# Linear attention with slots and eight experts on one core: roundings of batches 1 to 3 placed earlier, first loads and first two products woven

## The reference

```python
q, k, v = heads(x @ Wq), heads(x @ Wk), heads(x @ Wv)
s = clip(heads(x @ Ws), -32, 32)                  # 64 slots per head
z = cumlogsumexp(s); g = exp(z_before - z); p = exp(s - z)
hk = hk * g + k p^T;  ok = (q * scale) @ hk       # scan over tokens
pv = softmax(ok)
hv = hv * g + p v^T;  o = pv @ hv                 # scan over tokens
o = o * rsqrt(mean(o * o) + 1e-5) * g_norm * silu(x @ Wg)
x = layernorm(x + o @ Wo)
h = relu(x @ W1 + b1);  alpha = softmax(h @ W2 + b2)
x = layernorm(x + sum_k alpha_k * ((x @ V_k^T) @ U_k^T))
```

## Time and profile before

| | us |
|---|---|
| median of 3 runs | 1321.6 (1321.35 to 1323.63) |
| the profiled execution | 1321.39 |
| its span | 1319.6 |
| TensorE busy in it | 1304.1 (99%) |
| VectorE, ScalarE, GpSimd busy | 935.2, 534.8, 426.1 (71%, 41%, 32%) |

### The profile page before, as it was taken

One profiled execution on the slowest core, in us unless ns is written; L12 is line 12 of the kernel. 1 busy time (PEld: TensorE's weight loads), 2 busy tenths in 40 slices (PEclk: granted clock), 3 DMA queues, 4 the chain that ended last, 5 costly groups with the idle time before them and its releaser, 6 DMA issues.

```text
span 1319.6 us, 21997 instructions
## 1 busy us (share of the span) xinstructions
PE 1304.1 (99%) x8652; PEld 1151.3 (87%) x8652; DVE 935.2 (71%) x1887; ACT 534.8 (41%) x1551; POOL 426.1 (32%) x390
## 2 busy tenths in 40 slices
PE   9999999999999999999999999999999999999998
PEld 7888888898888888888888988888888888988886
DVE  5677777777777777777777777777777777766654
ACT  5434443444434433344334434444334433632321
POOL 3413342244223331334125422343123423442211
PEclk9999999999999999999999999999999999999999
DMA  6002100010000100010001000010000110000000
GB/s 231 33 32 65 49 17 1 1 45 13 17 1 25 33 17 1 19 39 17 1 1 49 9 17 1 24 33 17 1 25 25 65 34 1 1 0 33 31 34 33
DMA packets 33847, 36.04 MB, mean 27 GB/s; under 512 B 3536, under 2 KB 24016, under 8 KB 33744
## 3 DMA queue, kind: packets, MB, share of 16 engines
q1 hardware_dynamic: 33744, 34.64, 8.3%
HBM read 30.43 MB, written 4.19 MB: 26 GB/s over the span
## 4 chain that ended last, share of the span: by engine, by line
PE 95%; DVE 3%; ACT 1%; DMA 0%; issue 0%; SPq 0%; POOLq 0%; POOL 0%; DVEq 0%
PE p L1044 15%; PE p L1045 15%; PE p L1046 15%; PE t L1095 5%; PE o L1260 3%; PE s L1148 2%; PE xb L1213 2%; PE o L1198 2%; PE o L1196 2%; PE t L1260 2%; PE p L1148 2%; PE s L1572 2%; PE s L1573 2%; PE s L1574 2%; PE xb L1170 2%; PE o L1195 2%
## 5 line engine op out<-in xcount | busy, mean ns | idle before, releaser
L1044 PE MATMUL p<-wvg_hi,xt_hi 128*128 128x512 f32 x512 | 203.2, 397 | 0.0
L1045 PE MATMUL p<-wvg_lo,xt_hi 128*128 128x512 f32 x512 | 200.1, 391 | 0.0
L1046 PE MATMUL p<-wvg_hi,xt_lo 128*128 128x512 f32 x512 | 199.5, 390 | 0.0
L558 POOL TENSOR_TENSOR orstd<-ovar,minus_half 128x8 f32<-128x8 f32 x32 | 52.4, 1638 | 431.9 <-DVE ovar L995 431.9
L520 POOL TENSOR_TENSOR s_lo<-sums,s_hi 128x512 fp32r<-128x512 f32 x64 | 83.1, 1299 | 225.5 <-ACT s_hi L647 225.5
L1044 PE MATMUL p<-xt_hi,wsqk_hi 128*128 128x512 f32 x372 | 148.0, 398 | 2.1 <-DVE xt_lo L892 1.7
L1045 PE MATMUL p<-xt_lo,wsqk_hi 128*128 128x512 f32 x372 | 145.4, 391 | 0.0
L1046 PE MATMUL p<-xt_hi,wsqk_lo 128*128 128x512 f32 x372 | 145.1, 390 | 0.0
L622 ACT ACTIVATE v_tok<-p 128x256 f32<-128x256 f32 x128 | 49.6, 388 | 217.7 <-PE p L1046 216.7
L904 DVE COPY hv<-xb 64x128 f32<-64x128 f32 x192 | 55.1, 287 | 95.4 <-PE xb L1213 94.0
L1046 PEld LDWEIGHTS p<-wvg_hi,xt_lo 128*128 128x128 f32 x512 | 96.1, 188 | 20.9
(11 more groups left out here) (278 smaller groups left out, 3549.0 us busy)
## 6 DMA issues: line engine op xcount, KB each, us to landing
raw<-in_L_attn_Wv SPq DMA_DIRECT2D x32, 128.0 KB, 2.3
raw<-in_L_attn_Wg SPq DMA_DIRECT2D x32, 128.0 KB, 2.9
raw<-in_L_attn_Wo SPq DMA_DIRECT2D x16, 256.0 KB, 2.9
acc<-in_L_attn_hidden_states SPq DMA_DIRECT2D x4, 1024.0 KB, 5.6
out<-acc SPq DMA_DIRECT2D x16, 256.0 KB, 2.0
acc<-in_turned SPq DMA_DIRECT2D x3, 1024.0 KB, 8.9
raw<-in_L_attn_Ws SPq DMA_DIRECT2D x8, 256.0 KB, 2.9
raw<-in_L_attn_Wq SPq DMA_DIRECT2D x8, 256.0 KB, 2.9
```

Source lines behind the costliest of these rows:

```text
L558: nc.gpsimd.tensor_tensor(orstd[:], ovar[:], minus_half[:], ALU.pow).then_inc(orstd_done, 1)
L1044: nc.tensor.matmul(out_, lh, rh, start=(k == 0), stop=False)
L1045: nc.tensor.matmul(out_, lh, rl, start=False, stop=False)
L1046: last = nc.tensor.matmul(out_, ll, rh, start=False, stop=(k == n - 1))
```

## The change

The change has six parts. Nothing that is computed changes; eight transposes that fill time are left out.

1. SyncE issues the first loads woven: Ws, x tile 0, Wq, x tile 1, Wk, x tiles 2 and 3. ScalarE rounds them in that order; four pieces of Wv and Wg move by a place among the first features.
2. TensorE computes slots and queries together, tile by tile (`first_slots_and_queries`), with one group of four filling transposes instead of three. The transposes of e stand before the scores, and vg0 waits for the pieces of Wv and Wg one by one.
3. In cell 0, ScalarE rounds the last two groups of Wo behind the keys and then batch 2 (`x_high(act, 2)`); VectorE makes the second half of `xt_lo` of batch 1 before the exponential's result, the clip of the slots before `keep_values(2)`, and the first half of `xt_lo` of batch 2 at the cell's end.
4. In cell 1, ScalarE rounds batch 3 instead of batch 2; VectorE makes the second half of batch 2 where all four tiles stood, and the first half of batch 3 behind the additions. In cell 2 only the second half of batch 3 is left.
5. In the last cell `w2_low` moves behind the x1 tiles 1 to 3.
6. In the tail the four products of the last rows that go to p0 and p1 run before the wait for the hidden tile, and the two that go to OB after it.

```diff
         def sync_part(sp):
             xv = x.rearrange("b (n p) d -> b p n d", p=P)
             xtv = XT.rearrange("b (k p) t -> b p k t", p=P)
-            load_piece(sp, 0, name_of(0), 0)
             for kt in range(KT):
+                if kt < 3:
+                    load_piece(sp, 0, name_of(kt), kt)
                 sp.dma_start(acc[:, kt, :], xtv[0, :, kt, :]).then_inc(x0_in[kt], 16)
-            for i in (1, 2):
-                load_piece(sp, 0, name_of(i), i)
...
-        def rows_high(act, J):
-            act.wait_ge(wo_scaled, 2 * (J + 1))
-            if J > 0:
+        def rows_high(act, J, parts=range(4)):
+            if 0 in parts:
+                act.wait_ge(wo_scaled, 2 * (J + 1))
+            if 0 in parts and J > 0:
                 act.wait_ge(a_done, B * J)
-            for k, (where, src) in enumerate(row_groups):
+            for k in parts:
+                where, src = row_groups[k]
                 if k == 2:
                     act.wait_ge(wo_summed, 4 * (J + 1))
...
-        def x_high(act, b):
-            for kt in range(KT):
+        def x_high(act, b, parts=range(KT)):
+            for kt in parts:
                 act.wait_ge(*((x0_in[kt], 16) if b == 0 else (x_in[b], 16)))
                 nc.scalar.activation(xt_hi[b][:, kt, :], acc[:, b * CH + kt, :], ACT.Copy).then_inc(xt_hi_done, 1)
...
-            if 0 < cell.b < B - 1:
-                x_high(act, cell.b + 1)
+            if cell.b == 1:
+                x_high(act, 3)
...
-            if wo_J is not None:
+            if wo_J == 0:
+                rows_high(act, 0, (0, 1))
+            elif wo_J is not None:
...
+            if first(cell):
+                rows_high(act, 0, (2, 3))
+                x_high(act, 2)
...
         def scalar_part(act):
-            split_high(act, 0, 0, None)
-            x_high(act, 0)
-            split_high(act, 0, 1, None)
-            split_high(act, 0, 2, None)
+            for kt in range(KT):
+                if kt < 3:
+                    split_high(act, 0, kt, None)
+                x_high(act, 0, (kt,))
             split_high(act, 0, 3, None)
+            split_high(act, 0, 4, None)
             slots_scalar(act, Cell(None, 0))
+            split_high(act, 0, 5, None)
             queries_scalar(act, Cell(None, 0))
-            split_high(act, 0, 4, None)
-            split_high(act, 0, 5, None)
+            split_high(act, 0, 6, None)
             keys_scalar(act, Cell(None, 0))
-            split_high(act, 0, 6, None)
...
                                     ALU.subtract).then_inc(ok_less_top, 1)
-            if not first(cell):
+            if first(cell):
+                x_low(dve, 1, (2, 3))
+            else:
...
-                x_low(dve, cell.b + 1)
+                x_low(dve, cell.b + 1, (2, 3))
...
             keep_values(1)
-            if first(cell):
-                x_low(dve, 1, (2, 3))
             gate_vector(dve, cell, 3)
             if not first(cell):
                 add_c(dve, cell)
                 add_u3(dve, cell)
-            keep_values(2)
+            if cell.b == 1:
+                x_low(dve, 3, (0, 1))
             if cell.b == CELLS - 2:
                 dve.wait_ge(added, CELLS - B + 1)
                 car.norm1_tile(dve, 0, 0)
                 car.norm1_tile(dve, 0, 1)
+            if first(cell):
+                slots_vector(dve, nxt)
+                keep_values(2)
+                sums_vector(dve, nxt)
+                inverse_vector(dve, nxt)
+            else:
+                keep_values(2)
             if last:
-                car.w2_low(dve)
                 car.x_low(dve, 0, 0, X1[0])
-            if not last:
+            elif not first(cell):
                 slots_vector(dve, nxt)
                 sums_vector(dve, nxt)
                 inverse_vector(dve, nxt)
...
             if last:
                 for kt in range(1, KT):
                     car.x_low(dve, 0, kt, X1[kt])
+                car.w2_low(dve)
             if not last:
                 scores_kept(dve, nxt, 0)
                 scores_kept(dve, nxt, 1)
+            if first(cell):
+                x_low(dve, 2, (0, 1))
             if cell.b == CELLS - 2:
                 car.norm1_tile(dve, 0, 2)
                 car.norm1_tile(dve, 0, 3)
...
+        def first_slots_and_queries(pe, m, keep_warm):
+            banks = []
+            for use in "sq":
+                bk, before = p_turn(m.shifted(-1), use)
+                wait_read(pe, p_read, before)
+                banks.append(PB[bk])
+            for kt in range(KT):
+                for i, (bank_, done) in enumerate(zip(banks, (s_proj, q_proj))):
+                    if kt == 0:
+                        pe.wait_ge(w_hi_done, i + 1)
+                    if i == 0:
+                        pe.wait_ge(xt_hi_done, kt + 1)
+                    nc.tensor.matmul(bank_[:], wsqk_hi[:, i, kt, :], xt_hi[0][:, kt, :], start=(kt == 0), stop=False)
+                    if kt == 0 and i == 0:
+                        keep_warm(4)
+                    if kt == 0:
+                        pe.wait_ge(w_lo_done, i + 1)
+                    nc.tensor.matmul(bank_[:], wsqk_lo[:, i, kt, :], xt_hi[0][:, kt, :], start=False, stop=False)
+                    if i == 0:
+                        pe.wait_ge(xt_lo_done, kt + 1)
+                    mm = nc.tensor.matmul(bank_[:], wsqk_hi[:, i, kt, :], xt_lo[0][:, kt, :], start=False,
+                                          stop=(kt == KT - 1))
+                    if kt == KT - 1:
+                        mm.then_inc(done, 1)
...
             if c == 0 and first(cell):
-                pe.wait_ge(w_lo_done, 7)
+                for kt in range(KT):
+                    pe.wait_ge(w_lo_done, 4 + kt)
+                    first_pass, last_pass = kt == 0, kt == KT - 1
+                    nc.tensor.matmul(PB[bk][:], xt_hi[0][:, kt, 0:P], wvg_hi[:, kt, :], start=first_pass, stop=False)
+                    nc.tensor.matmul(PB[bk][:], xt_hi[0][:, kt, 0:P], wvg_lo[:, kt, :], start=False, stop=False)
+                    mm = nc.tensor.matmul(PB[bk][:], xt_lo[0][:, kt, 0:P], wvg_hi[:, kt, :], start=False, stop=last_pass)
+                mm.then_inc(vg_proj, 1)
+                return
...
+        def tail_rows_first(pe, h_done):
+            cell = Cell(None, CELLS)
+            for i in range(2):
+                part = (yt_hi[:, i, :, :], yt_lo[:, i, :, :])
+                bk, before = p_turn(cell, f"wo{i}")
+                wait_read(pe, p_read, before)
+                pe.wait_ge(yt_lo_done, CELLS * 2 - 1 + i)
+                row_product(PB[bk][:, 0:HALF], part, A12, B21, True, None)
+                row_product(PB[bk][:, HALF:D], part, A22, T4, True, m24_done)
+            pe.wait_ge(h_done, KT)
+            for i in range(2):
+                row_product(u_bank(cell)[:, i * HALF:(i + 1) * HALF], (yt_hi[:, i, :, :], yt_lo[:, i, :, :]), A11, B11,
+                            i == 0, m1_done if i == 1 else None)
...
+        def slots_turned(pe, cell):
+            pe.wait_ge(e_done, cell.count(1, 1))
+            turned(E_BANK, [e_t[:, cell.b % 2, tokens(c)] for c in range(CH)], e_turned)
...
-            feature_proj(pe, m, 0, s_proj, keep_warm)
-            feature_proj(pe, m, 1, q_proj)
+            first_slots_and_queries(pe, m, keep_warm)
             feature_proj(pe, m, 2, k_proj)
+            slots_turned(pe, m)
```

## The result

| | before | after |
|---|---|---|
| median | 1321.47 us (1321.28 to 1323.63, 4 runs) | 1314.19 us (1313.88 to 1314.76, 4 runs) |
| profiled execution, its span | 1321.39, 1319.6 | 1314.08, 1312.4 |
| TensorE busy | 1304.1 | 1302.7 |

The ratio is 0.9943, with a 95% interval of 0.9931 to 0.9956: faster by 7.3 us. The direction was right, the size was not: 7.3 instead of 4.2.

A forecast was written before the change was run, and what follows sets the result against it. The prediction took TensorE's own list of products as the bound; waits removed, -5.24, plus the head's +1.03 gave -4.2 from 1321.39, so 1317.2 us, with a whole range of 1315.9 to 1319.3.

The forecast's parts named there:

- The five waits: TensorE's waits in cell 0 (1.66, 0.69), cells 1 and 2 (1.06, 1.05) and tail (0.78) all go: -5.24 us.
- w2_low was worth nothing: Last cell: moving w2_low one place later brings 0, bounds -0.05 and +0.05, since the mask already starts when its scores are there.
- The push on hv: Cell 0: the moved xt_lo pair delays pz and the first hv copy by 0.4 to 0.8, costed at nothing.
- the load on ScalarE there: Cell 0: six copies, 3.8 us, behind k_t; squares 0 to 0.6 late, nothing on the path, 0.6 at worst.
- The clock: Rival, chance 0.03: TensorE stays at half rate after idling from about 7.0 to 8.7, giving 1328.5 us.
- The wait for the low part of Wq: First 20 us: one new TensorE wait of about 1 us near 8, low part there at 8.7 (8.4 to 9.25).
- The head: First 20 us: woven slots end later, so the first value product starts at 20.05 against 19.02, +1.0 (+0.3 to +1.9).
- cells 1 and 2: Two of four xt_lo tiles move elsewhere, so waits of 1.06 and 1.05 go whole, with 0.45 to spare.
- the remaining 0.4 for e_t near 1110 unchanged: Cell 30: TensorE's wait of 0.4 for e_t was expected to stay as it was.
- the scan: VectorE's scan in the first 20 us, between exponential and reciprocal: taken as 1.7 us, with 1.23 alone and 2.06 before.
- the head is free: Rival, chance 0.20: Wq lands at 6.4, scan undisturbed, chain 0.3 late or less; 1316.5 us, at best 1315.9.

The follow-up runs named there:

- Experiments 1 and 2: 1: kernel before with only keep_values(2) put behind the norm tiles in cell 30, 1319.93 us; 2: changed kernel with that edit undone, 1315.42 us.
- experiments 3: Kernel before with the edits of cells 0, 1 and 2 alone (loads, first products, cell 30, w2_low and tail as before): 1316.33 us.
- experiment 4: Changed kernel with the tail's wait for ht ahead of all twelve short products again, as before: 1314.82 us.
- experiment 6: Changed kernel with the old loads, roundings and first products, in two sessions: 1313.84 us, then 1313.78 beside the changed kernel's 1313.83.
- experiment 8: Changed kernel with the slot product one tile ahead of the query product in the woven head: 1314.2 us.
- experiment 7: Changed kernel with ScalarE rounding a piece of Wv and Wg ahead of the slots' exponential, so GpSimd runs when the scan starts: 1316.59 us.
- experiment 9: Changed kernel with the old loads and roundings, and slots computed tile by tile before the queries: 1313.64 us, then 1313.05 (ratio 0.9936).

## Why the prediction was off

**Right, step by step.** The five waits that it named all went. w2_low was worth nothing. In cell 0 the clip starts 2.66 earlier (38.23 for 40.89) where 2.6 was said. The push on hv and the load on ScalarE there cost nothing, also where the idle time of the earlier trace rows was used up whole. The clock stayed at its full level of 2.4 GHz (mean granted clock 0.999; products 0.23 apart from 8.6 on). The wait for the low part of Wq came as described (0.84 at 8.24). The head did cost and did not gain, along the chain that was described.

**Right with luck: cells 1 and 2.** The forecast had 0.45 to spare there, and the trace has nothing to spare. In cell 1 the two xt_lo tiles took 1.83 instead of 1.3 to 1.5, beside a GpSimd subtraction that starts with them (66.60 and 66.61); a part of the 3.03 for four tiles lay in the first two. In cell 2 they took 1.29, but VectorE came to them 0.5 later than before relative to TensorE: esq ahead of them took 0.69 instead of 0.17, while GpSimd was working too. A little more on VectorE there would have left a wait. (This is read off the traces; no run tested what made these operations longer.)

**The step that failed: cell 30 (-1.63).** The prediction said "the remaining 0.4 for e_t near 1110 unchanged". It read the one new place of keep_values(2) only where the change meant it, in cell 0, and took cell 30's wait for a fixed one. Experiments 1 and 2 show that this one line, alone, is worth 1.63 and nothing of it comes from elsewhere. The profile had it in plain sight: ww_t with two waits in the earlier trace rows, of which only one was placed, and e_t as a second wait in the same cell. It is also the largest part of the miss of 3.1.

**Mis-sized: the waits (-0.88).** Their terms were listed idle times, in sum 1.66 + 0.69 + 1.06 + 1.05 + 0.78 = 5.24. By starts they were worth 2.69 + 1.14 + 1.23 + 1.06 = 6.12; experiments 3 and 4 give 5.07 for the cells and 1.05 for the tail. A wait cost 0.1 to 0.3 more than its bracket. The first reason of experiment 4, a bracket that begins at the modelled end, can be read off at three more of them: from 34.61, 71.35 and 108.34 to the waiting matmul it was 2.26, 1.34 and 1.33 before, and 0.35, 0.14 and 0.13 in the same places after, so 1.91, 1.20 and 1.20 for brackets of 1.66, 1.06 and 1.05 (the last two are 1.14 and 1.23 in the table).

**Mis-sized: the head (+0.24 for +1.03).** Slots ended 0.14 earlier than said and the last links took 0.17 less; the rest, 0.48, is the scan: 1.22 where 1.7 was taken. The 0.14 hides two errors that nearly cancel: the product with the low part of Wq started at 8.24, ahead of the stated 8.4 to 9.25, and the 17 matmuls behind it took 0.35 more than 17 x 0.2275. And the +0.24 is itself the luck of one execution: by the table of experiment 6 the head costs 0.4 in the mean, and 0.87 in the other profile of this kernel. Only the scan is a settled miss: it took 1.22 or 1.23 in all six profiles in which it started ahead of GpSimd (those of the woven head and experiment 8), and 1.99 to 2.06 in all five with the old head, where it started second. The rival "the head is free" had this term right, yet its 1316.5 is still 2.4 above the 1314.1 of the profiled execution, for the reasons above.

For the scan, the rule that the prediction cited from the Trainium skill, page "SBUF — State Buffer", section "Who interferes with whom", was the better forecast. It has the engine that issues first keep the shared ports, and the changed kernel and experiment 7 show both orders: the one that starts first keeps its time within 0.03, the other stretches by 0.50 (GpSimd) or 0.69 (the scan). It is not quite the standstill of the rule, since the scan lost 0.69 of 0.83 overlapped.

The terms together: -1.63 - 0.88 - 0.79 + 0.21 (a drift over cells 3 to 31) = -3.1, the whole miss. The drift is 0.03 to 0.21 in all these kernels, and 0.21 and 0.07 in the two profiles of the changed kernel, so most of it differs between executions of one kernel; it gathers by about 0.01 a cell, and what makes it stays open.

## What to carry to other kernels

When a line moves in a loop body, read its new neighbours in every iteration whose branches differ, not only in the one that it was moved for: here the unplanned iteration gave a fifth of the gain. Price a TensorE wait by the distance of starts across it, less what that distance is without a wait, rather than by the bracket. And list every wait of the page that the forecast leaves standing, with the reason why it stays.

## What was not expected of the hardware

A transfer's landing in the first microseconds moves from execution to execution: Wq, third in line, was rounded at 5.42, 6.11, 6.17, 6.21, 6.83, 6.87 and 7.07 in the seven profiles of kernels that issue it in the same place, each time after ScalarE had waited for it, and the first tile of x at 4.4 to 5.7. In the woven order the first value product follows this (19.00 to 19.26 with Wq up to 6.21, 19.69 and 19.89 with it at 6.83 and 7.07). With the old order, where Wq is the sixth transfer and was rounded at 8.39 to 8.74, that product moved by 0.35.

Of the time that the scan and a GpSimd subtraction overlap, the one that came second lost most, but not all: the scan 0.69 of 0.83 (experiment 7) and 0.34 of 0.49 (experiment 9, beside an operation that ended at 11.77), GpSimd 0.50 of 0.66 (changed kernel) and 0.94 of 1.12 (experiment 9, the row of 11.73). Before the change the scan lost 0.83 of 0.97.
